# A two-layer decoder on one core: delta projections between the input projections, a four-step split of B and C, and cross-attention values made inside the state-space scan

## What is computed

```python
xr = layernorm(x) @ W_in;  u, res = xr[..., :256], xr[..., 256:]
u = silu(u)
delta = softplus(u @ W_delta + b_delta)
Bm, Cm = u @ W_B, u @ W_C                      # 16 states each
A = -exp(A_log)
h_t = exp(delta_t * A) * h_(t-1) + delta_t * B_t * u_t     # over 128 tokens
y_t = sum_n h_t[:, n] * C_t[n]
y = (y + u * D_param) * silu(res);  x = x + y @ W_out
# cross-attention behind it: q = layernorm(x) @ Wq + bq, k = ctx @ Wk + bk, v = ctx @ Wv + bv
```

## Time and profile before

| | |
|---|---|
| median of 3 runs | 940.71 us (937.53 to 940.95) |
| span of the profiled execution | 947.1 us |
| busy in it: TensorE, VectorE | 812.7 us (86%), 768.9 us (81%) |
| ScalarE, GpSimd | 524.0 us (55%), 492.0 us (52%) |
| mean granted TensorE clock | 0.952 |

### The profile page before, as it was taken

How to read it: one execution, slowest core, us unless ns; L and a number is a source line. 1 busy time by engine, 2 the same in 40 slices (tenths; PEclk the granted TensorE clock), 3 DMA queues, 4 the chain that set the end, 5 groups by cost and what they waited for, 6 DMA issues and landing times.

```text
span 947.1 us, 14667 instructions
## 1 busy us (share of the span) xinstructions
PE 812.7 (86%) x5061; PEld 583.1 (62%) x5061; DVE 768.9 (81%) x1419; ACT 524.0 (55%) x960; POOL 492.0 (52%) x490
## 2 busy tenths in 40 slices
PE   7958777777798999999999867799999899899891
PEld 6433232322266888887866555577766678789781
DVE  5588999999987489999848988886799978857663
ACT  5966666666637635554364232226565684078771
POOL 6358999999962021222248833456344310077773
PEclk9968999999998899999999999999799999999996
DMA  7000000000000031323000000000000031096554
GB/s 205 1 0 1 0 1 1 0 1 0 0 1 1 12 114 62 106 79 106 0 2 1 1 0 1 1 1 1 1 2 25 24 89 47 14 163 173 152 128 158
DMA packets 36739, 39.67 MB, mean 42 GB/s; under 512 B 5131, under 2 KB 28697, under 8 KB 35898
## 3 DMA queue, kind: packets, MB, share of 16 engines
q1 hardware_dynamic: 34170, 33.62, 11.8%
q0 software_dynamic: 2496, 5.12, 3.3%
HBM read 30.86 MB, written 7.86 MB: 41 GB/s over the span
## 4 chain that ended last, share of the span: by engine, by line
PE 39%; DVE 19%; ACT 5%; issue 5%; POOL 4%; DMA 3%; POOLq 0%; ACTq 0%; SPq 0%; DVEq 0%
PE ps L1751 10%; PE ps L1925 3%; PE ps L1744 3%; PE ps L2132 2%; DMA G<-xn_rows,token 2%; PE ps L1999 2%; PE ps L2267 2%; POOL y_rows L640 2%; DVE small L1520 2%; PE ps L2122 1%; PE ps L2276 1%; PE ps L2078 1%; DVE R L1481 1%; PE ps L1799 1%; DVE G L1523 1%
## 5 line engine op out<-in xcount | busy, mean ns | idle before, releaser
L1751 PE MATMUL ps<-xhl,whl 128*128 128x512 f32 x576 | 145.3, 402 | 5.3 <-ACT G L701 2.6
L1751 PEld LDWEIGHTS ps<-xhl,whl 128*128 128x128 f32 x576 | 109.0, 193 | 30.1 <-issue 5.7
L476 POOL TENSOR_TENSOR R<-G,R 128x1024 f32<-128x1024 f32 x43 | 100.8, 2360 | 28.9 <-ACT R L707 22.5
L1189 DVE TENSOR_TENSOR_SCAN R<-ps,R 128x1024 f32<-128x1024 f32 x43 | 97.5, 2278 | 5.5 <-POOL R L485 5.5
L749 ACT ACTIVATE ps<-G,negAb,negA 128x508 f32<-128x508 f32 x128 | 95.0, 779 | 2.6 <-DVE R L1189 2.6
L1778 PE MATMUL ps<-bc,sel 96*128 96x512 bf16 x128 | 47.1, 396 | 51.5 <-ACT LN L714 22.1
L1799 PE MATMUL ps<-R,ident 128*128 128x512 f32 x172 | 83.1, 605 | 0.0
L1778 PEld LDWEIGHTS ps<-bc,sel 96*128 96x128 bf16 x128 | 12.5, 99 | 104.7 <-ACT LN L714 35.8
L707 ACT COPY R<-ps 128x512 f32<-128x512 f32 x64 | 37.5, 585 | 71.1 <-PE ps L1778 71.1
L821 ACT ACTIVATE G<-ps 128x512 f32<-128x512 f32 x72 | 42.8, 599 | 56.7 <-PE ps L1751 56.6
L440 POOL TENSOR_TENSOR rstd<-small,mhalf 128x4 f32<-128x4 f32 x24 | 25.7, 1069 | 86.4 <-DVE small L1050 86.4
(11 more groups left out here) (376 smaller groups left out, 2162.8 us busy)
## 6 DMA issues: line engine op xcount, KB each, us to landing
R<-in_exp_wi_dram SPq DMA_DIRECT2D x39, 256.0 KB, 3.5
G<-cw_by_expert SPq DMA_DIRECT2D x6, 1024.0 KB, 4.6
ew<-in_w_dram SPq DMA_DIRECT2D x24, 128.0 KB, 2.2
y_rows<-zeros SPq DMA_DIRECT2D x1, 2048.0 KB, 9.3
xn_rows<-LN SPq DMA_DIRECT2D x8, 256.0 KB
G<-in_exp_wo_dram SPq DMA_DIRECT2D x8, 256.0 KB, 4.7
G<-y_rows SPq DMA_DIRECT2D x4, 512.0 KB, 5.5
X<-in_x_dram SPq DMA_DIRECT2D x4, 256.0 KB, 4.6
```

What stands on the lines that cost most here:

```text
L476: gp.tensor_tensor(halves(dBu[i % 3]), duT[:, :, gcols(i // NS)], Bsb[:, i % 4:i % 4 + 1, :].broadcast_to([P, HI, GT]), ALU.mult).then_inc ...
L1189: v.tensor_tensor_scan(hst[i % 3], bank(2 * j, 2).rearrange("p h n -> p (h n)"), dBu[i % 3], 0.0, ALU.mult, ALU.add).then_inc(S["scanned"], 1)
L1751: ins = mm(mix(out) if n == N_WIN1 else out, whl[:, wslot(n), i, m * P:(m + 1) * P], rhs, start=k == 0, stop=k == 2)
```

## The change

It has four parts. (1) The first layer norm is written out with another order on VectorE and ScalarE; GpSimd makes the lower part of W_in; VectorE zeroes `sel`, and GpSimd fills it once the last group is normalised; the silu table is loaded at the start. (2) The delta projections of groups 0 and 1 are put between the input projections, and those of groups 2 and 3 stay behind B and C. (3) B and C are computed three times over, on 96 rows, by weights `W_BC3` that VectorE lays out, and `bc_split` makes the three parts on VectorE alone, in four instructions a group placed between the softplus steps; ScalarE's logarithms follow the silus at once, and those of omega stand behind them. (4) Values (two sequences at a time) and folded query matrix are made in bank 4 inside the scan, in the steps of `VALUE_AT` and `WQK_AT`: TensorE issues them behind `c_row(i)`, ScalarE copies them out at the end of its step i, and `b_row(i+3)` follows that copy.

```diff
+VALUE_AT = (4, 6, 9, 12, 15, 17, 19, 22)
+WQK_AT = (25, 28)
...
-        bc_rest = lambda g: yT[0:2 * NS, 0, gcols(g)]
-        bc_mid = lambda g: yT[0:2 * NS, 1, gcols(g)].bitcast(BF16)[:, 0:GT]
+        bc_rest = lambda g: yT[0:4 * NS, 0, gcols(g)]
+        W_BC3 = G[:, 5, 0, 0:HI * 6 * NS].rearrange("p (h r n) -> p h r n", h=HI, r=3)
...
-            ln_scale(0)
+            ln_scale(0, (0,))
+            pool.wait_ge(S["w_upper"], 1)
+            gp.tensor_tensor(whl[:, wslot(0), 1], w["W_in"][:].rearrange("p m n -> p (m n)"), whl[:, wslot(0), 0].bitcast(F32),
+                             ALU.subtract).then_inc(S["w_split"], 1)
+            ln_scale(0, range(1, NG))
             gp.memset(ones[:], 1.0)
-            step(gp.memset(sel[:], 0.0))
+            wait(pool, "sel_zero", 1)
+            pool.wait_ge(S["ln_xn_b"], NG)
...
+            sc.preload_act_table_set("silu_and_others")
+            normalize(0, 0)
+            act.wait_ge(S["w_win"], 16)
+            sc.copy(whl[:, wslot(0), 0], w["W_in"][:].rearrange("p m n -> p (m n)")).then_inc(S["w_upper"], 1)
+            copy_xnT(0, 0)
+            normalize(0, 1)
+            silu_in(0, (0, 1))
+            normalize(0, 2)
+            copy_xnT(0, 1)
+            silu_in(0, (2, 3))
+            normalize(0, 3)
+            copy_xnT(0, 2)
+            copy_xnT(0, 3)
+            for g in range(1, NG):
+                silu_in(g)
...
+            for g in range(NG):
+                softplus_logs(g)
+                if g == 1:
+                    b_copy(0)
+
+            def v0_copy(k):
+                act.wait_ge(S["v_mm"], k + 1)
+                sc.copy(vS[0:LK, 2 * k:2 * k + 2, :], bank(4)[0:LK, 0, 0:2 * D].rearrange("p (b d) -> p b d", b=2)).then_inc(S["v_ev"], 1)
...
                         b_copy(i + 2)
                     if i >= 2 and on_pool(i - 2):
                         c_copy(i - 2)
+                    if i in VALUE_AT:
+                        v0_copy(VALUE_AT.index(i))
+                    elif i in WQK_AT:
+                        qk_copy(WQK_AT.index(i))
...
+            v.memset(sel[:], 0.0).then_inc(S["qk_mm"], 1)
...
             def bc_split(g):
-                wait(dve, "bc_up", min(2 * g + 3, 2 * NG))
-                v.tensor_tensor(bc3[64:96, gcols(g)], bc_rest(g), bc_mid(g), ALU.subtract).then_inc(S["bc_split"], 1)
+
+                dve.wait_ge(S["bc_mm"], g + 1)
+                src, two, low = bank(4 + g)[:, 0, :], slice(0, 4 * NS), slice(0, 2 * NS)
+                step(v.tensor_copy(bc3[:, gcols(g)], src[0:6 * NS]))
+                step(v.tensor_tensor(bc_rest(g), src[two], bc3[two, gcols(g)], ALU.subtract))
+                step(v.tensor_copy(bc3[two, gcols(g)], bc_rest(g)))
+                v.tensor_tensor(bc3[low, gcols(g)], bc_rest(g)[low], bc3[low, gcols(g)], ALU.subtract).then_inc(S["bc_split"], 1)
...
+            bc_split(0)
             softplus(0)
+            bc_split(1)
             delta_u(0)
             softplus(1)
             delta_u(1)
+            bc_split(2)
+            bc_split(3)
             softplus(2)
             first_column(0)
             delta_u(2)
             softplus(3)
             first_column(1)
...
             delta_u(3)
...
+            in_projection(0)
+            transpose_xn(0, 1)
+            delta_projection(0)
+            transpose_xn(0, 2)
+            transpose_xn(0, 3)
+            in_projection(1)
+            delta_projection(1)
+            in_projection(2)
+            in_projection(3)
+            pe.wait_ge(S["diag_ready"], 1)
...
-            def values(g):
-                if g >= 2:
-                    pe.wait_ge(S["v_ev"], g - 1)
-                for b in range(GB):
-                    ins = mm(bank(6 + g % 2)[0:LK, 0, b * D:(b + 1) * D], w["ctxT"][:, g * GB + b, :], w["Wv0"][:], start=True, stop=True)
+            def values(k):
+                pe.wait_ge(S["w_ctx"], 16 * 6)
+                pe.wait_ge(S["b_copied"], VALUE_AT[k] + 3)
+                for b in range(2):
+                    ins = mm(bank(4)[0:LK, 0, b * D:(b + 1) * D], w["ctxT"][:, 2 * k + b, :], w["Wv0"][:], start=True, stop=True)
                 ins.then_inc(S["v_mm"], 1)
...
             for i in range(NG * NS):
                 g, n = divmod(i, NS)
-                if i + 3 < NG * NS:
+                if i + 3 < NG * NS and i not in VALUE_AT + WQK_AT:
                     b_row(i + 3)
                 c_row(i)
+                if i in VALUE_AT:
+                    values(VALUE_AT.index(i))
+                elif i in WQK_AT:
+                    query_key_weights(WQK_AT.index(i))
...
                 if 2 <= i < NG * NS - 1:
                     y_sum(i - 2)
+                if i in VALUE_AT:
+                    pe.wait_ge(S["v_ev"], VALUE_AT.index(i) + 1)
+                    b_row(i + 3)
+                elif i in WQK_AT:
+                    pe.wait_ge(S["qk_ev"], WQK_AT.index(i) + 1)
+                    b_row(i + 3)
```

More of the change, by code:

```diff
@@ L736, in _, with qk_copy @@
                     sc.activation(d, d, ACT.Ln, bias=1.0).then_inc(S["sp_log"], len(ms))
-                    if g == NG - 1:
-                        b_copy(ms[0])
+                    if g == NG - 1 and ms[0] == 0:
+                        b_copy(1)
+            sc.preload_act_table_set("natural_log_exp_and_others")
+            act.wait_ge(S["w_mamba"], 16 * 7)
+            step(sc.activation(negA[:].rearrange("p h n -> p (h n)"), w["A_log"][:].rearrange("p h n -> p (h n)"), ACT.Exp))
+            sc.mul(negA[:].rearrange("p h n -> p (h n)"), negA[:].rearrange("p h n -> p (h n)"), -1.0).then_inc(S["omega_sp"], 1)
+            for g in range(NG):
[5 more added lines that the diff above has]
+                sc.copy(vS[0:LK, 2 * k:2 * k + 2, :], bank(4)[0:LK, 0, 0:2 * D].rearrange("p (b d) -> p b d", b=2)).then_inc(S["v_ev"], 1)
+            def qk_copy(k):
+                wait(act, "qk_up", k + 1)
+                if k == 0:
+                    sc.copy(WqkT[:], bank(4)[:, 0, 0:P + DC + 1]).then_inc(S["qk_ev"], 1)
+                else:
+                    sc.copy(Wqk[:], bank(4)[:, 0, 0:DC + 1])
+                    sc.copy(bqk[:], bank(4)[0:DC + 1, 0, P:P + 1]).then_inc(S["qk_ev"], 1)
+            step(sc.activation(coef[:, 1, :], w["omega"][:], ACT.Abs))
+            step(sc.activation(coef[:, 1, :], coef[:, 1, :], ACT.Exp, scale=-1.0))
+            sc.activation(coef[:, 1, :], coef[:, 1, :], ACT.Ln, bias=1.0)
             for g in range(NG):
@@ L1754, in _, with in_projection @@
             pe.wait_ge(S["const"], 1)
[L1756 to L1763 removed]
+            def in_projection(g):
                 pe.wait_ge(S["w_split"], 1)
@@ L1769, in _, with delta_projection @@
                     up(bank(4 + m)[:, 0, :], 0, m, g).then_inc(S["in_mm"], 1)
+            def delta_projection(g):
+                if g == 0:
+                    pe.wait_ge(S["w_mamba"], 16 * 7)
+                    pe.wait_ge(S["in_silu"], HI)
+                elif g == 1:
+                    pe.wait_ge(S["ln_lo"], NG)
+                    pe.wait_ge(S["in_silu"], 4 + HI)
+                for m in range(HI):
+                    if g == 0:
+                        pe.wait_ge(S["ln_lo"], m + 1)
+                    if g >= 2:
+                        pe.wait_ge(S["delta"], HI * (g - 2) + m + 1)
+                    for k in range(HI):
+                        ins = mm(bank(2 * (g % 2) + m)[:, 0, :], w["W_delta"][:, k, m * P:(m + 1) * P], uT[:, k, gcols(g)],
+                                 start=k == 0, stop=k == HI - 1)
+                    ins.then_inc(S["dl_mm"], 1)
+            unread(7, 18)
+            transpose_xn(0, 0)
+            unread(7, 5)
+            in_projection(0)
[8 more added lines that the diff above has]
+            pe.wait_ge(S["diag_ready"], 1)
             for g in range(NG):
@@ L1773, in _ @@
                 for k in range(HI):
-                    ins = mm(bank(4 + g)[0:2 * NS, 0, :], w["W_BC"][:, k, :], uT[:, k, gcols(g)], start=k == 0, stop=k == HI - 1)
+                    ins = mm(bank(4 + g)[0:6 * NS, 0, :], W_BC3[:, k].rearrange("p r n -> p (r n)"), uT[:, k, gcols(g)],
+                             start=k == 0, stop=k == HI - 1)
                 ins.then_inc(S["bc_mm"], 1)
@@ L1801, in y_sum @@
                 ins.then_inc(S["y_acc"], 1)
-            for g in range(NG):
-                for m in range(HI):
-                    if g >= 2:
-                        pe.wait_ge(S["delta"], HI * (g - 2) + m + 1)
-                    for k in range(HI):
-                        ins = mm(bank(2 * (g % 2) + m)[:, 0, :], w["W_delta"][:, k, m * P:(m + 1) * P], uT[:, k, gcols(g)],
-                                 start=k == 0, stop=k == HI - 1)
-                    ins.then_inc(S["dl_mm"], 1)
-                if g == NG - 2:
-                    pe.wait_ge(S["const"], 2)
-                    pe.wait_ge(S["bc_split"], NG)
-                    b_row(0)
```

123 lines of the change are left out of this document (39 added, 84 removed).

## The result

The changed kernel takes 971.64 us (median of 4 runs, 966.28 to 977.8) against 939.38 for the kernel before (4 runs beside it, 937.53 to 940.95). The ratio is 1.0346, 95% interval 1.0316 to 1.0377: 32.3 us slower, where 21.5 were forecast. The profiled execution has a span of 975.8 us.

A forecast was written before the change was run, and what follows sets the result against it. A ring of latencies across engines, with VectorE having 0.53 us of room every 9.42 us, was taken as the scan's bound. 947.1 - 2.4 (front) + 23.9 (scan) = 968.6, +21.5; carried to the median 940.71: 962.2 us, eight-in-ten range 949 to 972.

The forecast's parts named there:

- The mechanism of the hold: In ten scan steps VectorE waits for a serial chain: c_row, value matmuls, ScalarE's copy, then decay(i+1), before scan(i+1).
- the sign: Whole kernel: slower than before by over 0.5%, with chance 0.90.
- Rival 1: In the scan: the inserted work is hidden by idle ScalarE, only the front counts, 938.3 us; chance 0.08.
- The term for the scan: Inside the scan: ten holds of VectorE lose 23.9 us together, bounds 19 to 31.
- The hold itself: Step 9 of the scan as example: scan(10) starts 2.77 us behind hc(8) instead of 0.53.
- No second wait: Behind each hold: b_row(i+3) comes about 2.8 us later, its drive wanted over 7 us after, so nothing more lost.
- rival 3: In the scan: TensorE's clock falls to half because of the holds, 994 us; chance 0.07.
- The term for the front: Ahead of the scan: first scan at 60.9 instead of 63.33, 2.4 us won; bounds 8 won, 1 lost.
- GpSimd's holds: Ahead of the scan: GpSimd's three drives hold VectorE's instructions for 4.8 us, bounds 0 and 7.1.
- Half absorbed (950): In the scan: half of each hold is absorbed, 1.2 us a step left, 950 us; chance 0.12.
- The front loses (965): Ahead of the scan: splits and holds push the first scan past 63.33, 1 us lost, 965; within the forecast's range.
- No effect: Whole kernel: the new values wait isn't met where placed, and the time differs by less than 0.5%; chance 0.02.

The follow-up runs named there:

- experiment 1: Changed kernel with ScalarE's copy of the values or query matrix moved behind decay(i+1); 950.9 us, ratio 1.0107.
- experiment 2: Kernel of experiment 1 with TensorE's b_row(i+3) put straight behind the value copy, ahead of the y_sum; 937.59 us, ratio 0.9984.
- experiment 5: Changed kernel with 14 small matmuls adding zeros on TensorE in the step behind eight of the ten holds; 964.19 us, ratio 1.0255.
- 6: Changed kernel with the values made in four steps of four sequences instead of eight of two; 959.46 us, ratio 1.0217.
- 8: Kernel before with only values and query matrix moved into the scan, copy behind decay(i+1), b_row ahead of the sums; 939.54 us, ratio 0.9999.
- Experiment 9: Kernel of experiment 2 with unread matmuls added on TensorE ahead of and into the first scan steps; 937.75 us, ratio 0.9973.

## Why the prediction was right, and where it was not

**The mechanism of the hold and the sign** were right. The serial chain is there link by link, ten times, and the loss ends where the last query step ends. Experiments 1 and 2 show it from the other side: with the copy behind the decay and b_row ahead of the sum the scan costs 2 to 5 us more than before instead of 41. Rival 1 (hidden, 938) was dismissed because c_row(i) stands ahead of the values. In experiment 2 it still does, and the time is 937.6: what forbade the hiding was the copy's place ahead of decay(i+1), and then b_row's behind the sum. The Trainium skill (Perfetto Trace Analysis, "Optimizing Scalar/DVE Operations") suggests moving work from a full VectorE to an emptier ScalarE; in this trace ScalarE was idle a third of the time, and the move cost 32.3 us as it was placed, none in experiment 2. Its idle share was there, but not at that point of its queue.

**The term for the scan, 23.9 us, was mis-sized**; it measured 41.1. The parts, as far as the runs separate them:
- The hold itself: 2.93 us where 2.77 were worked out. c_row(9) starts 0.24 behind hc(8), not 0.06, because of the y_sum ahead of it. For the two query steps (25, 28) 1.9 and 2.1 were assumed, and experiments 5 and 6 show 2.62 for both. In experiment 5, with the clock mostly up, the ten holds less the 2.9 us of gaps that the same steps had before are 27.6, that is 3.7 over the forecast, some of it still by the clock's fall between 110 and 150.
- The second waits at full clock, seven of 0.28 to 0.58 in experiment 5: 2.55 us, where the length of its scan leaves 2.3 for them. "No second wait" was wrong: b_row(i+3) comes late by less than its slack, as I said, but it shares TensorE's queue with the y_sum and the next c_row, and ScalarE's copy of C stands behind b_copy; hc waits for the c_row behind both.
- The clock, 11.2 us: the difference in length between the changed kernel's scan (241.2) and experiment 5's (230.1). It is likely too low, as two holds had no fillers and the clock was 0.91 there.

So the step that failed is the one that left the clock to rival 3 alone, all or nothing (994). It stood neither at 1.00 nor at 0.50: it fell and rose within each group of holds. "The prediction is wrong if the granted clock in the scan isn't 1.00" came true as far as the size goes: 0.67 to 0.92 in the stretches between 80 and 190 us. The case of a partly lost clock, forecast plus a third of rival 3's 32 us, would have given 973, close to the 971.64 measured, and was not among the cases. That the range of 949 to 972 held the median, by 0.4 us, was luck: its upper end was the sum of the largest holds, and the front paid for what the clock took.

**The term for the front, 2.4 us, was mis-sized** too; it measured 5.7, and the first scan at 57.64 lies outside the 59 to 62 that were to show the mechanism. Of the 3.3 us, 1.4 are GpSimd's holds (3.4, costed at 4.8), 1.2 the splits (2.5 us a group instead of 2.8, as the third step takes 0.42), and 0.5 the start (32.38 instead of 32.9). The order was right: but for 0.53 us at 35.77 VectorE's queue is full from 32.4 us to the first scan. The zeroing of `sel` cost nothing, where 0.4 was taken. The memset is over at 3.05, and the statistics start at 3.89, 0.24 behind those of before:

```profile
1.29 1.76 DVE L1129 MEMSET sel<- 96x2048 uint32 x1 [1.29 <-PEq L2373]
...
3.89 0.87 DVE L1071 BATCH_NORM_STATS2 stats<-X 128x6 f32<-128x128 f32 x4 [0.84 <-DMA X<-in_x_dram]
...
10.47 3.02 PE L1768 MATMUL ps<-xhl,whl 128*128 128x512 f32 x12 [0.66 <-DVE xhl L1093]
```

VectorE waited for data in between, so the 0.24 is the data's and not the memset's. The first input projection came at 10.47, where 10.2 was forecast.

**The other rivals.** Half absorbed (950): no, the scan lost more than the holds alone, and behind step 32 it runs at 9.42 us for three steps as before, so nothing was made up. The front loses (965): no. No effect: no.

**The expectations of the experiments** missed where an order was improved: 944 against 950.9, 934 against 937.59, 935.6 against 939.54. Each time the wait that I removed uncovered the next one in another in-order queue, which I had costed too low or at nothing: b_row behind the sum in experiment 1, the gate behind y_sum(15) in 2 and 8.

## What to carry to other kernels

When work goes to an engine that is idle a third of the time, ask what is queued behind it there, not how idle the engine is: a copy of 0.37 us ahead of the next step's exponentials cost VectorE about 2.4 us or more in each of ten steps, and behind them, with the next queue put right too, 2 to 5 us for all ten. Do the same for the second queue: what is issued late because it waits for that copy must stand ahead of long work on its own engine. And where a change puts idle time into TensorE's stream, cost the clock as a part of each hold, since every matmul behind it may run at half speed.

## What the runs showed of the hardware

- TensorE's granted clock fell to between 0.67 and 0.90 of 2.4 GHz in the five stretches of 20 us from 90 to 190, where TensorE was busy 12.8 to 15.0 us; four matmuls of 512 columns took 3.62 us instead of 1.88 behind an idle wait of 2.33. Adding 3.29 us of useless matmuls to eight steps made the kernel 7.4 us faster (971.64 to 964.19), and the four matmuls behind each of the two holds without them still took 3.30 and 3.44.
- It doesn't follow busy time alone. In experiment 9 it fell to 0.83 in a stretch with 15.86 us busy of 20, where the same stretch of experiment 2 had 15.73 us and 1.00 (matmuls at half clock count as busy for longer).
- A cast from SBUF to SBUF took 0.42 us where the step that reads PSUM took 0.68, and was held to 1.14 beside GpSimd's drive; in no group were the three steps with 0.67 to 0.69 held. The Trainium skill (SBUF — State Buffer, "Who interferes with whom") says that VectorE is held by GpSimd when it has two SBUF inputs or runs a copy or cast in a two-port mode. The trace agrees, with the held product (2.37 us against 0.74) and the held cast. The steps that read PSUM ran beside a drive (46.97 to 49.53) at 47.25 and 47.96 and took 0.67 and 0.68. The fourth step, with both inputs in SBUF, met a drive once, in the third group, and was ahead of it: it started at 46.65 and took its 0.68, while the drive that began at 46.97 took 2.56 instead of 2.37.
- Zeroing 96 x 4096 bfloat16 elements took VectorE 1.76 us as 2048 words of uint32, and GpSimd 3.51 as 4096 bfloat16 elements.
